# Attention of a post-norm block on one core: score blocks, transposing tasks and value products in clusters, q and k projected two groups ahead, biases waited for one by one

## What is computed

```python
qkv = einsum('bsd,ed->bse', x, w_qkv) + b_qkv            # 16 heads of 32
scores = einsum('bhqd,bhkd->bhqk', q, k) / sqrt(32) + causal mask
out = einsum('bhqk,bhkd->bhqd', softmax(scores), v)
x = layernorm(x + einsum('bsd,ed->bse', out, w_out) + b_out)
# then, with integer weights (w - 128) * scale and 2048 hidden features
x = layernorm(x + (silu(x Wg^T) * (x Wu^T)) Wd^T)
```

## Time and profile before

| | |
|---|---|
| median of 3 runs | 824.63 us (824.39 to 826.4) |
| the profiled execution | 824.49 us |
| its span, first to last instruction | 822.7 us |
| mean granted TensorE clock | 0.989 of full |
| busy: PE, PE's weight loads | 791.6 us (96%), 577.0 us (70%) |
| busy: DVE, ACT, POOL | 416.7 us (51%), 382.2 us (46%), 95.7 us (12%) |
| chain that ended last, by engine | PE 91%, DVE 3%, ACT 2%; SPq, DMA and issue 1% each |

### The profile page before, as it was taken

One profiled execution on the slowest core, in us unless ns is written; L12 is line 12 of the kernel. 1 busy time (PEld: TensorE's weight loads), 2 busy tenths in 40 slices (PEclk: granted clock), 3 DMA queues, 4 the chain that ended last, 5 costly groups with the idle time before them and its releaser, 6 DMA issues.

```text
span 822.7 us, 12318 instructions
## 1 busy us (share of the span) xinstructions
PE 791.6 (96%) x4672; PEld 577.0 (70%) x4672; DVE 416.7 (51%) x1038; ACT 382.2 (46%) x914; POOL 95.7 (12%) x87
## 2 busy tenths in 40 slices
PE   5899999999999999999899999999999999999994
PEld 4666666666666666666578888878887888878883
DVE  2656755666556655666754333254324532264226
ACT  2457666667566666566724444342223223232220
POOL 0000031005300133003432000000000000000001
PEclk9899999999999999999999999999999999999998
DMA  9100221113111150110654333010210011000201
GB/s 317 67 1 1 88 68 52 52 53 137 68 52 52 52 194 14 52 52 14 219 161 135 115 115 128 1 53 14 77 65 0 0 38 64 0 1 14 90 0 53
DMA packets 34311, 56.09 MB, mean 68 GB/s; under 512 B 7248, under 2 KB 7248, under 8 KB 34256
## 3 DMA queue, kind: packets, MB, share of 16 engines
q1 hardware_dynamic: 34256, 55.34, 20.3%
HBM read 46.94 MB, written 8.39 MB: 67 GB/s over the span
## 4 chain that ended last, share of the span: by engine, by line
PE 91%; DVE 3%; ACT 2%; SPq 1%; DMA 1%; issue 1%; POOLq 0%; POOL 0%; DVEq 0%; ACTq 0%
PE bank L1203 14%; PE bank L1204 14%; PE bank L1075 9%; PE bank L1209 7%; PE bank L1210 7%; PE bank L1019 6%; PE bank L1038 6%; PE bank L1061 6%; PE bank L1096 5%; PE bank L1000 4%; PE bank L1002 4%; PE bank L1004 4%; PE bank L1189 2%; ACT probs L602 1%; PE bank L1107 1%; DMA bias_o<-in_L_attn_b_out_dram 1%
## 5 line engine op out<-in xcount | busy, mean ns | idle before, releaser
L602 ACT ACTIVATE probs<-probs,neg_max 128x128 f32<-128x128 f32 (+3 forms) x256 | 140.6, 552 | 34.1 <-DVE neg_max L766 34.1
L880 DVE SCALAR_TENSOR_TENSOR hid<-bank,u_scale,silu 128x512 f32<-128x512 f32 x64 | 48.0, 750 | 182.1 <-PE bank L1204 178.3
L766 DVE CUSTOM_DVE_ANT_0 probs<-bank,causal 128x128 f32<-128x128 f32 (+3 forms) x256 | 111.5, 486 | 39.5 <-PE bank L1061 38.4
L1075 PEld LDWEIGHTS bank<-ident,probs 128*128 128x128 f32 x640 | 73.6, 141 | 46.9 <-issue 30.3
L1209 PE MATMUL bank<-downT,hid_hi 128*128 128x512 f32 x256 | 103.0, 402 | 2.7 <-DVE hid_lo L883 2.7
L1203 PE MATMUL bank<-xT_hi,gateT 128*128 128x512 f32 x256 | 102.6, 401 | 0.0
L1210 PE MATMUL bank<-downT,hid_lo 128*128 128x512 f32 x256 | 101.5, 397 | 0.0
L1204 PE MATMUL bank<-xT_lo,gateT 128*128 128x512 f32 x256 | 100.7, 393 | 0.0
L1075 PE MATMUL bank<-ident,probs 128*128 128x128 f32 x640 | 98.8, 278 | 1.8 <-ACT probs L602 1.7
L1204 PE MATMUL bank<-xT_lo,upT 128*128 128x512 f32 x256 | 100.3, 392 | 0.0
L1203 PE MATMUL bank<-xT_hi,upT 128*128 128x512 f32 x256 | 100.3, 392 | 0.0
(11 more groups left out here) (88 smaller groups left out, 1180.3 us busy)
## 6 DMA issues: line engine op xcount, KB each, us to landing
z_tok<-in_L_attn_x_dram SPq DMA_DIRECT2D x4, 1024.0 KB, 5.5
scan_buf<-in_L_ffn_gate_w_dram SPq DMA_DIRECT2D x4, 1024.0 KB, 5.5
scan_buf<-in_L_ffn_up_w_dram SPq DMA_DIRECT2D x4, 1024.0 KB, 5.4
scan_buf<-in_L_ffn_down_w_dram SPq DMA_DIRECT2D x4, 1024.0 KB, 5.3
y_scratch<-z_tok SPq DMA_DIRECT2D x16, 256.0 KB, 2.0
x_tok<-y_scratch SPq DMA_DIRECT2D x4, 1024.0 KB, 6.7
w_int<-in_L_ffn_gate_w_dram SPq DMA_DIRECT2D x16, 256.0 KB, 4.6
w_int<-in_L_ffn_up_w_dram SPq DMA_DIRECT2D x16, 256.0 KB, 2.7
```

Of the source, the lines that this page charges most:

```text
L602: nc.scalar.activation(probs[qb][:, j, :], probs[qb][:, j, :], ACT.Exp, bias=neg_max[:, qb, j:j + 1], scale=-1.0, accum_out=row_sum[:, qb, ...
L766: nc.vector.tensor_tensor_reduce(out=probs[qb][:, j, :], in0=score[j][:, 0:w], in1=causal[:, S - w:S], scale=-SCALE, scalar=-FLOOR, op0=AL ...
L1075: last = nc.tensor.transpose(acc[:, m * P:(m + 1) * P], probs[qb][:, j, kb * P:(kb + 1) * P], ident[:, :])
```

## The change

Each score block, task and value product keeps its work; the tables move them. Blocks 0 and 1 of the next group's scores are computed together, in one bank per head side by side, at step 6; tasks stand in pairs at steps 0, 8, 10, 12; value products in pairs at 6, 12 and the next group's step 0. The jobs' products stand in clusters of 4 to 12. q and k are projected two groups ahead, so the other jobs move too, and groups 1 and 2 get 48 and 36 products, group 14 gets 12. The inverse is taken in two halves. Transposes of x go to steps 5 and 7, two weight tiles from group 1 to group 2, the scans to groups 3 to 10. POOL adds b_out at g = 0 of the next batch, and after the last group before its last `att_lo`. SP does its stores of y1 and the load of z_tok at g = 3. In the front the second weight tile comes after x, its first scores come together, q and k run all products hi x hi first and wait for the parts of each third on their own, and each bias has its semaphore.

The diff, cut (semaphore names, the bank tables' and the loops' new look-ups and the same step changes of ACT left out):

```diff
@@ -41,9 +41,12 @@
     STEPS = 16
-    SCORE_STEPS = {0: (0, 2), 3: (0, 3), 9: (1, 0), 12: (1, 1)}
-    MAX_STEPS = {s + n: (ahead, qb, (2 * n, 2 * n + 1)) for s, (ahead, qb) in SCORE_STEPS.items() for n in range(2)}
-    EXP_STEPS = {s + n: (ahead, qb, (2 * n - 2, 2 * n - 1)) for s, (ahead, qb) in SCORE_STEPS.items() for n in (1, 2)}
+    SCORE_STEPS = {0: (0, (2,)), 3: (0, (3,)), 6: (1, (0, 1))}
+    PER_GROUP = len(SCORE_STEPS)
+    MAX_STEPS = {0: (0, 2, (0, 1)), 1: (0, 2, (2, 3)), 3: (0, 3, (0, 1)), 4: (0, 3, (2, 3)),
+                 6: (1, 0, (0, 1, 2, 3)), 7: (1, 1, (0, 1)), 8: (1, 1, (2, 3))}
+    EXP_STEPS = {1: (0, 2, (0, 1)), 2: (0, 2, (2, 3)), 4: (0, 3, (0, 1)), 5: (0, 3, (2, 3)),
+                 8: (1, 0, (0, 1)), 9: (1, 0, (2, 3)), 10: (1, 1, (0, 1)), 11: (1, 1, (2, 3))}
@@ -53,20 +56,20 @@
...
-    TASK_STEPS = [0, 2, 3, 7, 8, 10, 11, 12, 13, 14]
+    TASK_STEPS = [0, 0, 3, 8, 8, 10, 10, 12, 12, 15]
     PRODUCTS = [(0, 1), (2,), (3, 4), (5, 6), (7, 8), (9,)]
-    PRODUCT_STEPS = [4, 5, 10, 13, 15, STEPS]
-    INVERSE_STEP = 13
+    PRODUCT_STEPS = [6, 6, 12, 12, STEPS, STEPS]
+    INVERSE_STEP = 15
     SLOTS = 6
-    X_STEPS = [8, 9, 10, 11]
-    SCAN_STEPS = [7, 15]
+    X_STEPS = [5, 5, 7, 7]
+    SCAN_STEPS = [6, 14]
...
-    W_STEPS = {(0, 6): 8, (0, 11): 9, (1, 5): 10, (1, 8): 11, (1, 9): 12, (1, 11): 13, (1, 13): 14, (1, 15): 15}
+    W_STEPS = {(0, 5): 8, (0, 7): 9, (1, 5): 10, (1, 7): 11, (1, 9): 12, (1, 11): 13, (2, 9): 14, (2, 11): 15}
@@ -78,22 +81,40 @@
...
-    EVEN = [0, 5, 4, 1, 4, 4, 5, 4, 4, 3, 2, 4, 2, 1, 3, 2]
-    AROUND_X = [0, 4, 4, 1, 4, 4, 4, 3, 0, 0, 3, 4, 4, 4, 5, 4]
-    FIRST_HALF = [0, 4, 4, 1, 4, 4, 4, 3] + [0] * 8
+    LAST = B - 1
+    EVEN = [4, 0, 0, 8, 0, 0, 8, 0, 4, 0, 6, 0, 6, 0, 0, 12]
+    AT_FRONT = [12, 0, 0, 12, 0, 0, 6, 0, 6, 0, 6, 0, 6, 0, 0, 0]
     def filling(G):
         b, g = divmod(G, NG)
-        jobs = [("q", G + 1), ("k", G + 1)] if G + 1 < GROUPS else []
+        ahead = [("q", G + 2), ("k", G + 2)] if G + 2 < GROUPS else []
         if G == 0:
-            return jobs + [("v", 0, 2), ("v", 0, 3)], EVEN
-        if g < 2 and b > 0:
-            return jobs + [("o", b - 1, QH * g + t) for t in range(QH)], EVEN
-        if g == 2 and b + 1 < B:
-            return jobs + [("v", b + 1, t) for t in range(QH)], AROUND_X
-        if g == 3 and b + 1 < B:
-            return jobs + [("v", b + 1, QH + t) for t in range(QH)], EVEN
-        return (jobs, FIRST_HALF) if jobs else ([], [0] * STEPS)
+            return [("q", 1), ("k", 1), ("v", 0, 2), ("v", 0, 3)], AT_FRONT
+        if G == 1:
+            return [("q", 2), ("k", 2)] + ahead, AT_FRONT
+        if g == 0:
+            return [("v", b, NT - 1)] + ahead + [("o", b - 1, 0)], EVEN
+        if g == 1:
+            return [("o", b - 1, 1), ("o", b - 1, 2)] + ahead, EVEN
+        before = [("o", b - 1, NT - 1)] if g == 2 and b > 0 else []
+        values = [] if b == LAST else [("v", b + 1, 0)] if g == 2 else [("v", b + 1, 1), ("v", b + 1, 2)]
+        jobs = before + values + ahead
+        counts, skip = list(EVEN), (0 if before else MM) if g == 2 else 0
+        for s in range(STEPS):
+            taken = min(skip, counts[s])
+            counts[s], skip = counts[s] - taken, skip - taken
+            left = MM * len(jobs) - sum(counts[:s])
+            counts[s] = max(0, min(counts[s], left))
+        return jobs, counts
@@ -184,11 +205,10 @@
...
-    SCAN_FIRST = 2
+    SCAN_FIRST = 3
@@ -406,15 +428,17 @@
...
-            load_w(1)
             load_x(2)
             load_x(3)
+            load_w(1)
             with nc.allow_non_contiguous_dma(reason="a bias per partition"):
-                sp.dma_start(bias_qk[:, :], b_qkv[0:2 * D].rearrange("(c p) -> p c", p=P)).then_inc(bias_loaded, 16)
-            sp.dma_start(bias_v[:, :], b_qkv[2 * D:3 * D].partition_broadcast(P)).then_inc(bias_loaded, 16)
-            for i in range(2, NW):
+                sp.dma_start(bias_qk[:, :], b_qkv[0:2 * D].rearrange("(c p) -> p c", p=P)).then_inc(bias_qk_loaded, 16)
+            for i in range(2, 8):
                 load_w(i)
-            sp.dma_start(bias_o[:, :], b_out.partition_broadcast(P)).then_inc(bias_loaded, 16)
+            sp.dma_start(bias_v[:, :], b_qkv[2 * D:3 * D].partition_broadcast(P)).then_inc(bias_v_loaded, 16)
+            for i in range(8, NW):
+                load_w(i)
+            sp.dma_start(bias_o[:, :], b_out.partition_broadcast(P)).then_inc(bias_o_loaded, 16)
             sp.dma_start(z_tok[:, :, :], x_v[0]).then_inc(z_loaded, 16)
@@ -455,20 +479,20 @@
...
-                if g == 2 and b > 0:
+                if g == 2 and b + 2 <= B:
+                    load_x_ahead(b + 2)
+                if g == 3 and b > 0:
                     store_y1(b - 1)
                     sp.wait_ge(y1_stored, b * (16 * NT))
                     sp.dma_start(z_tok[:, :, :], x_v[b]).then_inc(z_loaded, 16)
-                if g == 2 and b + 2 <= B:
@@ -541,27 +564,29 @@
...
-                wait_alone(pool, inv_done, G + 1)
+                wait_alone(pool, inv_done, 2 * (G + 1))
...
+            def add_bias(b):
+
+                pool.wait_ge(bias_o_loaded, 16)
+                pool.wait_ge(z_loaded, b * 16 + 16)
+                for t in range(NT):
+                    last = nc.gpsimd.tensor_tensor(z_tok[:, t, :], z_tok[:, t, :], bias_o[:, :], ALU.add)
+                last.then_inc(res_ready, 1)
...
-                if g == 2 and b > 0:
-                    for t in range(QH):
-                        apply_norm(b - 1, t)
                 widen_inverse(G)
                 if g == 2 and b > 0:
-                    for t in range(QH, NT):
+                    for t in range(NT):
                         apply_norm(b - 1, t)
-                if g == 3:
-
-                    pool.wait_ge(z_loaded, b * 16 + 16)
-                    for t in range(NT):
-                        last = nc.gpsimd.tensor_tensor(z_tok[:, t, :], z_tok[:, t, :], bias_o[:, :], ALU.add)
-                    last.then_inc(res_ready, 1)
+                if g == 0 and b > 0:
+                    add_bias(b - 1)
+            add_bias(LAST)
             att_lo(GROUPS - 1)
@@ -627,39 +652,37 @@
...
-            w_hi(1)
...
-            w_hi(2)
-            w_hi(3)
-            for j in range(HG):
-                exponential(0, 0, j)
-            w_hi(4)
-            w_hi(5)
-            for j in range(HG):
-                exponential(0, 1, j)
+            for i in range(1, 6):
+                w_hi(i)
+            for qb in range(QH):
+                for j in range(HG):
+                    exponential(0, qb, j)
...
+                    if s == 0 and G > 0:
+                        keep_inverse(G - 1)
...
-                    if s == INVERSE_STEP + 1:
-                        keep_inverse(G)
...
+            keep_inverse(GROUPS - 1)
             att_hi(GROUPS - 1)
@@ -762,14 +785,16 @@
...
+                first = P_WIDTH[0] if qb == 1 else 0
+                dve.wait_ge(score_full[j], G * PER_GROUP + max(qb - 1, 0) + 1)
                 nc.vector.tensor_tensor_reduce(
-                    out=probs[qb][:, j, :], in0=score[j][:, 0:w], in1=causal[:, S - w:S], scale=-SCALE, scalar=-FLOOR,
+                    out=probs[qb][:, j, :], in0=score[j][:, first:first + w], in1=causal[:, S - w:S], scale=-SCALE, scalar=-FLOOR,
...
-            def inverse_sum(G):
-                dve.wait_ge(exp_done, (G + 1) * NT * HG)
-                nc.vector.reciprocal(inv_sum[:, :, :], row_sum[:, :, :]).then_inc(inv_done, 1)
+            def inverse_sum(G, hf):
+                qbs = slice(QH * hf, QH * (hf + 1))
+                dve.wait_ge(exp_done, (G * NT + QH * (hf + 1)) * HG)
+                nc.vector.reciprocal(inv_sum[:, qbs, :], row_sum[:, qbs, :]).then_inc(inv_done, 1)
@@ -822,20 +847,21 @@
...
-            w_lo(1)
             x_lo(0, 2)
             x_lo(0, 3)
-            dve.wait_ge(bias_loaded, 16 * 3)
+            w_lo(1)
+            dve.wait_ge(bias_qk_loaded, 16)
             take(("q", 0))
             take(("k", 0))
             w_lo(2)
+            w_lo(3)
             for j in range(HG):
                 tile_max(0, 0, j)
-            w_lo(3)
             w_lo(4)
             w_lo(5)
             for j in range(HG):
                 tile_max(0, 1, j)
+            dve.wait_ge(bias_v_loaded, 16)
@@ -850,17 +876,20 @@
...
-                    if s == 6:
-                        inverse_sum(G)
-                    if g == 2 and s in X_STEPS:
-                        x_lo(b + 1, X_STEPS.index(s))
+                    if s == 2:
+                        inverse_sum(G, 0)
+                    if s == 9:
+                        inverse_sum(G, 1)
...
-                    if g == 2 and s == 1 and b > 0:
+                    if g == 2 and s == 5 and b > 0:
@@ -988,21 +1017,30 @@
...
-                for c in range(ND):
-                    first, final = c == 0, c == ND - 1
```

(69 more changed lines are left out.)

53 lines of the change are left out of this document (28 added, 25 removed).

## The result

The kernel after takes 858.25 us (median of 4, 855.42 to 861.26) against 824.76 for the kernel before beside it: ratio 1.0403 [1.0363, 1.0443], 33.5 us slower. Forecast were 838.0 and a range up to 850. The direction is right, the size is not: slower by two and a half times the forecast, outside the range.

What follows compares the result with a forecast made beforehand. PE's own sequence was taken to bound the plain groups. Terms -8.2 - 23.8 + 41.3 + 2.6 + 2.8 - 1.2 = +13.5 us on a median of 824.63 gave 838.0 us, range 827 to 850.

Steps and rivals of the forecast that it cites:

- Rival B: Granted clock falls too at the new waits in the groups: five times 2.4 us, 850 us, possibly 870; chance 14%.
- Part 3: Small terms: bank waits +2.6 us over 13 groups, twelve more products +2.8, group 1's idle -1.2; groups 14 and 15 0.
- The new wait at step 6: PE waits for all 16 maxima before the next group's scores, behind DVE's ended job: 2.1 us, 3.2 behind an output.
- Part 1: Clusters in groups 0 to 13: joined scores and paired value products save 1.7 us per group, -23.8 us; paired tasks nothing.
- Part 2: PE's stalls for maxima before scores, mainly at step 6, with related waits in groups 0 to 13: together +41.3 us.
- rival C: Faster: DVE reaches the last two maxima before the job's end, so step 6 stalls vanish: 808 us; chance 11%.
- Rival D: No change: savings of 1.9 per group, no bank waits, a front of 9.5: 828 us and just under; chance 7%.
- Part 4: The front: bias and x_lo waits go, values start at 19.9 instead of 28.14, -8.2 us.

Runs made afterwards that it cites:

- the maxima first: Kernel after with one swap on DVE: at steps 1 and 4 the maxima come before the job that ended; 814.67 us, ratio 0.9857.
- banks apart: Kernel after with maxima before ended jobs, plus 3 or 4 products between weight or x transposes and tasks in groups 0-2, 6, 10, 14; 808.45 us.

## Why the prediction was wrong, by its own steps

Two steps failed. Rival B's reason, that waits between dense work leave the clock alone, was wrong: the new waits brought it down eight times, some 11 us. And Part 3 priced the waits for banks too low: 6.4 us in groups 0 to 2 stand in no term. The new wait at step 6, which the forecast rested on, was right.

**Part 1, right.** In the kernel after two value products stand in 0.79 us (55.66 to 56.45: 0.64 and one 0.15 on the way), which settles that nothing drains between two of them. PE's timeline of the kernel after, group 1:

```profile
54.64 1.09 PE L1118 MATMUL bank<-ident,probs 128*128 128x128 f32 x8
55.66 0.86 PE L1139 MATMUL bank<-probsT,v_tok 128*32 128x256 f32 x16
56.45 0.50 PE L1042 MATMUL bank<-xT_hi,wT_hi 128*128 128x512 f32 x1
```

The joined scores of step 6 hold PE 0.87 (67.99 to 68.86). The pairs measured 0.9 a group where 1.05 was put. Of the whole 1.7 a plain group shows 1.4 (24.13 before, 22.97 with the maxima first, of which 0.27 is a wait). Neither the rest nor the share of the joined scores was tested by itself.

**Part 2, right in groups 3 to 14.** The waits at step 6 are 2.09 (forecast 2.1), 3.09 (3.2) and 2.22 (2.3). A plain group at full clock is 24.80, +0.67 where the terms give +0.6. In groups 0 and 1 the waits for maxima are 1.79 and 1.72, 7.0 in both groups where 7.2 was put. Group 10, which has no fall, is +2.2 (28.53 against 26.32), where the terms give +1.8.

**Part 3, too small: the waits for banks in groups 0 to 2.** "+2.6 over 13 groups" priced one job behind two tasks, and only in the usual order; the weight tiles and the transposes of x that now stand next to pairs of tasks were not counted through. Eight waits there that no term held, 1.07 three times, 0.98 twice, 0.33, 0.44 and 0.50, sum to 6.4 us. Groups 0 to 2 came out +14.0, their terms give +7.5: in the sum that is the difference, though single groups are off by up to 1.0. Spacing the fills (banks apart) took 4.6 of them away. It also sizes rival C: 808 was given for the case without stalls, and the kernel with the maxima first, which is that case, takes 814.67. Rival D's list (savings of 1.9, no waits for banks, a front of 9.5) gives 831 and not 828; that decided nothing.

**Part 3, behind the groups: taken as 0, measured +1.4.** The 0 stood for groups 14 and 15, which came 0.5 shorter with a fall in them, and for the last `att_lo`. That one stands behind the additions of the bias, and they wait 4.85 us for z_tok. POOL's timeline of the kernel after, and PE's behind it:

```profile
445.13 5.59 POOL L576 TENSOR_TENSOR z_tok<-z_tok,bias_o 128x512 f32<-128x512 f32 x4 [4.85 <-DMA z_tok<-in_L_attn_x_dram]
450.69 1.44 POOL L562 TENSOR_TENSOR attT_lo<-attT,attT_hi 128x512 fp32r<-128x512 f32 x1
```

```profile
452.18 0.50 PE L1076 MATMUL bank<-wT_hi,attT_hi 128*128 128x512 f32 x1 [1.14 <-POOL attT_lo L562]
```

With the maxima first z_tok comes in time for PE, and this wait is not there.

**Part 4, right, to the digit by luck.** The values start at 19.94 (19.9) and the front gives 8.2 us. With the same front group 0 starts at 25.72 to 29.81 in the profiles of the other kernels made from this one, so one execution gives 4.9 and another 9.0. What is late next is w_lo, as the step said:

```profile
19.94 0.47 PE L1057 MATMUL bank<-wT_hi,xT_hi 128*128 128x512 f32 x1 [1.79 <-DVE wT_lo L762]
```

**Rival B, the step that failed most.** It was given 14%, and against it stood only "they lie between dense work". They do, and the clock falls all the same: after the 3.09 of groups 5, 9 and 13 every time, after 2.22 in two of three groups, after 2.09 in one of six. Group 5 runs at 0.63 for 9 us, 6.7 us of half clock, and two such stretches lie in group 13 too; with one each in 3, 6, 9 and 14 that is eight. At 1.2 to 1.6 each, from pairs of equal groups (3 against 7, 6 against 10, 5 against 9), it comes to some 11 us as an estimate, and the comparison with the maxima first gave 1.4 each. The rival's own price, 2.4 a fall, was too high, since it came from a stretch twice as long; its count, five, too low; that its sum of 12 was near is luck, as the two errors cancel. The earlier trace rows had been fair evidence: in the front PE idled for 2.7 us before the clock fell, and the longest new waits were above that. The kernel before had closer evidence, which the forecast does not use: in its feed-forward part, amid dense work, PE waits 1.93 us and the granted clock is at half (1.2 GHz) right behind. PE's timeline of the kernel before and a stretch of it:

```profile
537.75 0.50 PE L1209 MATMUL bank<-downT,hid_hi 128*128 128x512 f32 x1 [1.93 <-DVE hid_lo L883]
```

```profile
539.00:542.00 3.00, 3.00 (x9) 2.33 (x8) 3.00 (x6) 2.76 (x4) 0.00 (x0) 0.50 0.77 298
```

The ledger against the forecast's +13.5, in spans: 11 for the clock (an estimate), 6.5 for the banks of groups 0 to 2, 1.4 behind the groups and 0.3 of smaller terms make the +32.7 measured. No single one would have left the range; B's 850 had the clock with everything else as forecast, so it missed when a second term came on top.

## What to carry to other kernels

When a change pulls a consumer closer to its producer, write down the order of the instructions on the engine between them: here a job that waits for the last product stood ahead of two maxima whose input was long there, and swapping them is worth 43.6 us at no cost. Price the clock with a wait on TensorE, inside dense work too: here 18 of 33 waits of 2.1 to 2.9 us cost some 1.5 us more for it, and all eight of over 3 us did. And gather only what changes the array's tiling: pairs of value products save 0.9 us a group, pairs of transposes on the full array nothing, and a pair behind a transposed weight or x tile made PE wait about 1 us for a bank.
